# First layer of an eight-stage network: bit unpacking in 16-bit halves, three leaf buffers, codes on VectorE, row sums on TensorE

## The reference, cut to what matters

```python
def fake_quant(x, scale, zp):
    q = jnp.clip(jnp.round(x / scale + zp), 0.0, 255.0)
    return (q - zp) * scale
x = x + jnp.matmul(fake_quant(layernorm(x), s1, z1), fake_quant(ctx, s2, z2))

for p in range(4):                       # plane p holds bit p of each 4-bit code
    bits = (qweight[p][:, :, None] >> shifts & 1).reshape(O, I)
    idx = idx | bits << p
w = jnp.take_along_axis(lut4, idx, axis=1)          # dense weight (512, 512)
x = x + jnp.einsum('bsi,oi->bso', layernorm(x), w) + bias
```

## Time and profile before

| | us |
|---|---|
| median of 3 runs | 890.11 |
| lowest, highest | 885.03, 890.35 |
| the profiled execution, its own time | 884.34 |
| its span in the profile | 882.6 |

### The profile page before, as it was taken

How to read it: one execution, slowest core, us unless ns; L and a number is a source line. 1 busy time by engine, 2 the same in 40 slices (tenths; PEclk the granted TensorE clock), 3 DMA queues, 4 the chain that set the end, 5 groups by cost and what they waited for, 6 DMA issues and landing times. The chain is left out here.

```text
span 882.6 us, 16392 instructions
## 1 busy us (share of the span) xinstructions
PE 784.0 (89%) x5130; PEld 632.8 (72%) x5130; DVE 722.5 (82%) x1712; ACT 518.0 (59%) x1410; POOL 448.2 (51%) x391
## 2 busy tenths in 40 slices
PE   0886699948978899999999999999999999678978
PEld 0366576634657888888888888888888888465446
DVE  7788898977777797897897897897897897974975
ACT  6683788845437557657657657657657657331431
POOL 4727259815134745745745745845844844713110
PEclk9898999989989999999999999999999999989899
DMA  8333146635120320320320320320320320203001
GB/s 313 129 112 116 45 162 213 201 102 168 26 71 1 96 73 1 96 71 0 95 71 0 95 71 0 95 71 0 95 71 0 95 72 0 72 25 116 1 0 48
DMA packets 39114, 68.23 MB, mean 77 GB/s; under 512 B 5729, under 2 KB 18593, under 8 KB 38946
## 3 DMA queue, kind: packets, MB, share of 16 engines
q1 hardware_dynamic: 39074, 67.73, 23.5%
HBM read 62.38 MB, written 5.34 MB: 77 GB/s over the span
## 5 line engine op out<-in xcount | busy, mean ns | idle before, releaser
L2218 DVE TENSOR_SCALAR_CACHE_REDUCE xn<-ctxT,candidate 128x512 bf16<-128x512 f32 x248 | 174.4, 740 | 0.1
L1950 ACT ACTIVATE layer_attention_probs<-xnT,stats 128x512 f32<-128x512 f32 x128 | 93.9, 734 | 135.1 <-DVE stats L2058 135.1
L1734 PE MATMUL bank<-layer_attention_keysT,layer_attention_queriesT 128*128 128x512 f32 x384 | 123.9, 431 | 3.3 <-DVE layer_attention_queriesT L2051 3.3
L2070 DVE TENSOR_TENSOR layer_attention_probsT<-bank,layer_attention_probsT 128x512 fp32r<-128x512 f32 x128 | 88.0, 688 | 40.3 <-ACT layer_attention_probsT L1958 38.9
L1734 PEld LDWEIGHTS bank<-layer_attention_probsT,layer_attention_values 128*128 128x128 f32 x768 | 99.7, 191 | 19.4 <-issue 9.1
L1734 PE MATMUL bank<-layer_attention_probsT,layer_attention_values 128*128 128x256 f32 x768 | 103.1, 284 | 10.3 <-DVE layer_attention_probsT L2070 9.9
L1734 PE MATMUL bank<-layer_attention_wo,layer_attention_headsT 128*128 128x512 f32 x384 | 102.1, 409 | 3.9 <-issue 3.1
L1958 ACT CAST layer_attention_probsT<-bank 128x512 fp32r<-128x512 f32 x128 | 74.7, 584 | 51.1 <-PE bank L1809 51.1
L1681 POOL TENSOR_TENSOR layer_attention_mixed<-layer_attention_mixed,xnT 128x512 f32<-128x512 f32 x32 | 52.3, 1633 | 86.8 <-DMA xnT<-inverse_sums 84.5
L1734 PE MATMUL bank<-layer_attention_l_wq,layer_attention_xnT 128*128 128x512 f32 x384 | 93.7, 393 | 0.7 <-DVE layer_attention_xnT L2119 0.7
L1734 PE MATMUL bank<-layer_attention_l_wkv,layer_context_parts 128*128 128x256 f32 x720 | 90.4, 278 | 0.0
(11 more groups left out here) (318 smaller groups left out, 1690.6 us busy)
## 6 DMA issues: line engine op xcount, KB each, us to landing
layer_attention_l_raw_qo<-in_wqT SPq DMA_DIRECT2D x9, 1024.0 KB, 5.0
xnT<-inverse_sums SPq DMA_DIRECT2D x16, 512.0 KB, 3.7
layer_attention_l_raw_qo<-in_woT SPq DMA_DIRECT2D x8, 1024.0 KB, 7.0
tw_raw<-in_w_gateT SPq DMA_DIRECT2D x8, 688.0 KB, 5.3
tw_raw<-in_w_upT SPq DMA_DIRECT2D x8, 688.0 KB, 4.2
tw_raw<-in_w_downT SPq DMA_DIRECT2D x6, 768.0 KB, 4.7
layer_attention_l_raw_kv<-in_wkvT SPq DMA_DIRECT2D x9, 512.0 KB, 5.0
ternary<-tw_rounded SPq DMA_DIRECT2D x8, 344.0 KB, 2.5
```

The lines of the kernel that those rows point to most:

```text
L1734: last = pe.matmul(out, stationary[f][a], moving[f][b], start=f == 0 and x == 0, stop=f == count - 1 and x == 2)
L1950: a.activation(probs[:, u % 3, :], masked[:, u % 2, :], ACT.Exp, bias=negmax[:, u:u + 1], scale=-1.0, accum_out=sums[:, u:u + 1]).then_inc ...
L2070: v.tensor_tensor(probsT[:, 1, p % 2, :, columns], T[u % 2][:, :].rearrange("p (c q) -> p c q", c=CPB), probsT[:, 0, p % 2, :, columns], A ...
L2218: own(k.nc.vector.tensor_scalar(k.flags[:, r % 2], row_tile(k.ctxT, r), k.candidate[:, r:r + 1].bitcast(F32), 0.0, ALU.is_gt, ALU.add, acc ...
```

## The change

- The packed planes are read as 16-bit halves. `unpack(b)` for b in 0 to 15 takes bit b of every half of all four groups in one shift-and-mask; `bits` is 16-bit, holds all groups at once and is laid out bit-major, and the second norm writes `xn` in the same order of features (`norm_rows(..., HALVES)`). All 16 run before the statistics of x. `shifts`, `moved` and the iota are gone.
- `tree` has three buffers. Leaves: group 0 five by ScalarE and three by GpSimd (ahead of the norm's power in its queue), groups 1 and 2 by ScalarE, group 3 four and four. A small activation loads ScalarE's table early.
- The codes q1 and q2 are made by VectorE, each right behind its rounding. The row sums of the codes come from TensorE (`row_sums`, sixteen products with one column) and not from ScalarE; its rectifying of ctx is interleaved with the copies of q1T.
- The bias is cut into two float32r parts by GpSimd, and added by two products per tile.
- ScalarE's order behind x corrected: leaves(1), weightT_copy(0), leaves(2), xnT copies, leaves(3), wv, first keys copy, then the ternary sums with the weightT copies between them, the second keys copy before sum 7. `keys(1)` is TensorE's last work in the layer, and its two subtractions VectorE's last. `cols` lies in `ctx` and `bias` in `xnT`.

```diff
-def norm_rows(k, n):
+def norm_rows(k, n, halves=None):
...
+        to, source = k.xn[:, t, :], k.x[:, t, :]
+        if halves is not None:
+            to, source = to.rearrange("p (b h) -> p h b", h=halves), source.rearrange("p (h b) -> p h b", h=halves)
...
+    HALVES, HALF_BITS = 2 * WORDS, BITS // 2
+    BUFFERS = 3
+    BY_POOL = {0: 5, 3: 4}
...
+        planes = packed[:, 0:OT * PLANES * WORDS].bitcast(U16).rearrange("p (a h) -> p a h", h=HALVES)
...
-        bits = k.sbuf("bits", [P, 2, PLANES, D], I32, s)
+        bits = k.sbuf("bits", [P, OT, PLANES, D], U16, s)
+        by_bit = bits[:, :, :, :].rearrange("p o a (b h) -> p (o a) b h", h=HALVES)
...
+                    for j in range(BY_POOL[o], CODES // 2):
+                        last = g.tensor_scalar(tree[:, o % BUFFERS, j, :], bits[:, o, 0, :], diff[:, o, j:j + 1],
...
+                leaves(0)
                 norm_gpsimd(k, n)
-                for t in range(TILES):
-                    g.wait_ge(S_["x_rounded"], t + 1)
-                    g.tensor_scalar(q1[:, t, :], k.xn[:, t, :], 1.0, -(ROUND + MIDDLE), ALU.mult, ALU.add)\
-                     .then_inc(S_["q1_ready"], 1)
-                context_codes(0)
-                context_codes(1)
-                leaves(1, 0, CODES // 2, "leaves1_pool")
+                g.wait_ge(S_["bias_loaded"], 16)
+                g.wait_ge(S_["constants_ready"], 5)
+                g.tensor_copy(ones_row[:, :], k.ones[0:1, :]).then_inc(S_["bias_low"], 1)
+                g.tensor_copy(bias_parts[:, 0, :], bias).then_inc(S_["bias_high"], 1)
+                g.wait_ge(S_["bias_high"], 1)
+                g.tensor_tensor(bias_parts[:, 1, :], bias, bias_parts[:, 0, :], ALU.subtract).then_inc(S_["bias_low"], 1)
                 norm_gpsimd(k, n + 1)
-                leaves(3, 0, 4, "leaves3_pool")
+                leaves(3)
...
-                def unpack(o):
...
+                def unpack(b):
+                    v.tensor_scalar(by_bit[:, :, b, :], planes, b, 1, ALU.logical_shift_right, ALU.bitwise_and)\
+                     .then_inc(S_["bits_ready"], 1)
...
-                unpack(0)
+                for b in range(HALF_BITS):
+                    unpack(b)
+                v.wait_ge(S_["bits_ready"], HALF_BITS)
                 v.wait_ge(k.x_loaded, 16)
                 norm_statistics(k)
-                unpack(1)
                 norm_rows(k, n)
                 for t in range(TILES):
...
+                    v.wait_ge(S_["x_rounded"], t + 1)
+                    v.tensor_scalar(q1[:, t, :], k.xn[:, t, :], 1.0, -(ROUND + MIDDLE), ALU.mult, ALU.add)\
+                     .then_inc(S_["q1_ready"], 1)
...
                 norm_statistics(k)
-                unpack(2)
-                norm_rows(k, n + 1)
+                norm_rows(k, n + 1, HALVES)
                 choose(1)
-                unpack(3)
                 choose(2)
                 choose(3)
...
+                keys_low(0)
...
                 tile_norms_vector(k, following, update)
+                keys_low(1)
...
                 a.wait_ge(S_["diff_ready"], 1)
+                a.activation(corr[:, :], lut[:, 0, 0:TILES], ACT.Identity).then_inc(S_["table_loaded"], 1)
                 leaves(0)
...
-                rectified_context(0)
-                rectified_context(1)
...
-                    a.activation(junk[:, t % 2, :], q1[:, t, :], ACT.Copy, accum_out=rows[:, t:t + 1]).then_inc(S_["rows_ready"], 1)
...
+                for t in range(TILES):
+                    rectified_context(t)
+                    if t % 2:
+                        turned_codes(t - 1)
+                        turned_codes(t)
+                for t in range(CPB, CTILES):
+                    rectified_context(t)
...
+                leaves(1)
                 weightT_copy(0)
-                for i in range(3):
-                    ternary_sums_scalar(k, i)
+                leaves(2)
...
-                leaves(2)
-                weightT_copy(1)
-                ternary_sums_scalar(k, 3)
-                leaves(3, 4)
-                ternary_sums_scalar(k, 4)
+                leaves(3)
                 a.wait_ge(lw.ctx_loaded, 32)
                 a.copy(lw.wv[:, :], lw.raw_v[:, :]).then_inc(lw.wv_high, 1)
...
+                keys_copy(0)
+                ternary_sums_scalar(k, 0)
+                weightT_copy(1)
+                ternary_sums_scalar(k, 1)
+                ternary_sums_scalar(k, 2)
                 weightT_copy(2)
-                for i in range(5, 7):
-                    ternary_sums_scalar(k, i)
+                ternary_sums_scalar(k, 3)
+                ternary_sums_scalar(k, 4)
                 weightT_copy(3)
+                ternary_sums_scalar(k, 5)
+                ternary_sums_scalar(k, 6)
+                keys_copy(1)
                 ternary_sums_scalar(k, 7)
...
+                def row_sums():
+                    pe.wait_ge(S_["q1T_ready"], TILES)
+                    for t in range(TILES):
+                        for f in range(KT):
+                            last = pe.matmul(ROWS[:, t:t + 1], q1T[:, f, t * P:(t + 1) * P], ones16[:, 0:1],
+                                             start=f == 0, stop=f == KT - 1)
+                    last.then_inc(S_["rows_psum"], 1)
...
-                        pe.matmul(Y[t][:, :], k.ones[0:1, 0:P], bias[0:1, :], start=True, stop=False, skip_group_check=True)
+                        for part in range(2):
+                            pe.matmul(Y[t][:, :], ones_row[:, :], bias_parts[:, part, :], start=part == 0, stop=False,
+                                      skip_group_check=True)
...
+                row_sums()
                 columns(0)
...
-                pe.wait_ge(S_["weightT_ready"], 1)
-                keys(1)
                 feed_forward(1)
...
                 feed_forward(3)
+                pe.wait_ge(S_["weightT_ready"], OT)
+                keys(1)
```

More of the change, by code:

```diff
@@ L449, in layer0 @@
         d2s = k.sbuf("d2s", [P, 1], F32, s)
-        rows = k.sbuf("rows", [P, TILES], F32, s)
         corr = k.sbuf("corr", [P, TILES], F32, s)
         ones16 = k.sbuf("ones16", [P, P], BF16, s)
-        cols = k.sbuf("cols", [1, B, D], F32, s)
-        junk = k.sbuf("junk", [P, 2, D], BF16, s)
-        shifts = k.sbuf("shifts", [P, BITS], I32, s)
-        moved = k.sbuf("moved", [P, PLANES * WORDS, BITS], I32, s)
-        bits = k.sbuf("bits", [P, 2, PLANES, D], I32, s)
+        cols = ctx[0:1, 0:B, :]
@@ L500, in _ @@
                 g.wait_ge(S_["constants_ready"], 1)
-                def leaves(o, first, end, done):
-                    g.wait_ge(S_["bits_ready"], o + 1)
-                    if o >= 2:
-                        g.wait_ge(S_["weightT_psum"], o - 1)
-                    for j in range(first, end):
-                        last = g.tensor_scalar(tree[:, o % 2, j, :], bits[:, o % 2, 0, :], diff[:, o, j:j + 1],
-                                               lut[:, o, 2 * j:2 * j + 1], ALU.mult, ALU.add)
-                    last.then_inc(S_[done], 1)
@@ L606, in _, with keys_low @@
                 norm_statistics(k)
[L607 to L608 removed]
+                norm_rows(k, n + 1, HALVES)
                 choose(1)
[L610 removed]
                 choose(2)
                 choose(3)
[L613 to L615 removed]
+                def keys_low(b):
                     v.wait_ge(lw.keys_high, b + 1)
@@ L631, in _, with leaves @@
             def _(a):
-                def leaves(o, first=0):
-                    a.wait_ge(S_["bits_ready"], o + 1)
-                    if o >= 2:
-                        a.wait_ge(S_["weightT_psum"], o - 1)
-                    for j in range(first, CODES // 2):
-                        last = a.activation(tree[:, o % 2, j, :], bits[:, o % 2, 0, :], ACT.Identity,
+                def leaves(o):
+                    a.wait_ge(S_["bits_ready"], HALF_BITS)
+                    if o >= BUFFERS:
+                        a.wait_ge(S_["weightT_psum"], o - BUFFERS + 1)
+                    for j in range(BY_POOL.get(o, CODES // 2)):
+                        last = a.activation(tree[:, o % BUFFERS, j, :], bits[:, o, 0, :], ACT.Identity,
                                             bias=lut[:, o, 2 * j:2 * j + 1], scale=diff[:, o, j:j + 1])
@@ L648, in scaled_columns, with rectified_context, turned_codes @@
                     a.activation(cols[0:1, b, :], C[b][0:1, :], ACT.Copy, scale=off[0:1, 0:1]).then_inc(S_["cols_ready"], 1)
-                def rectified_context(b):
-                    a.wait_ge(S_[f"ctx{b}_loaded"], 16)
-                    for t in range(b * CPB, (b + 1) * CPB):
-                        a.activation(ctx[:, t, :], ctx[:, t, :], ACT.Relu, bias=par[:, 3:4], scale=inv[:, 1:2])\
-                         .then_inc(S_["ctx_rectified"], 1)
+                def rectified_context(t):
+                    a.wait_ge(S_[f"ctx{t // CPB}_loaded"], 16)
+                    a.activation(ctx[:, t, :], ctx[:, t, :], ACT.Relu, bias=par[:, 3:4], scale=inv[:, 1:2])\
```

(6 more changed lines are left out.)

88 lines of the change are left out of this document (35 added, 53 removed).

## The result

| | before | changed |
|---|---|---|
| median, us (6 runs each) | 887.08 | 878.31 |
| lowest, highest | 885.03, 890.35 | 876.66, 882.09 |
| profiled execution, its span | 884.34, 882.6 | 877.61, 875.9 |

The ratio is 0.990, with a 95% interval of 0.987 to 0.993. The time lies 6.2 us under the forecast of 884.5 and 0.2 under the low end of the range.

A forecast was written before the change was run, and what follows sets the result against it. The prediction took a chain that changes engine in layer0, the only stage touched, as the bound. Its terms, 2.1 + 1.2 + 3.7 - 1.4 = 5.6 us, took the median from 890.11 to 884.5, range 878.5 to 891.

The forecast's parts named there:

- the anchor: Whole kernel: the median before, 890.11 us, from which the forecast subtracted the saving; the profiled execution lay 5.8 under it.
- part B: Layer0, norm's rows to scaled_columns(1): 1.2 us saved, with TensorE's row sums at 2.1 setting the stage.
- A, start to R: Layer0's opening: 16 unpack operations at 0.23 us and a power without its wait save 2.1 us.
- R: The start of the norm's rows in layer0, forecast at 12.1 us against 14.17 before.
- The rival with the f32 rate: Unpack in layer0's opening at 0.37 us per operation: 2.2 us worse, 886.7; at 0.61, 890.6; chance 0.18.
- C, to the last products: Layer0, scaled_columns(1) to the last products: ScalarE's 23.5 us, then waits for ternary pieces; 3.7 us saved.
- D, to layer1: Last products to layer1: keys(1)'s two subtractions now stand behind the norm; 1.4 us lost.
- The mask: Rival: VectorE's choosing gets slower from a 16-bit mask for f32 data; at double price 895.3 us; chance 0.06.
- the clock's: Rival: TensorE's products before layer1 run at clock 0.50, up to 3.8 us more per group, 892; chance 0.06.
- The length from layer1 on: Sign: everything from layer1 on shifts whole; a change by more than 2 us would show the prediction wrong.
- the three open prices: Row sums (limited to 1.4 us), fetches under 4.0 (0.8 at most) and layer1's first transposes less cold (1.2).
- TensorE's side goes better: Rival: row sums, fetches and layer1's first transposes all cheaper, 9.0 us saved, 881.1; chance 0.2.

The follow-up runs named there:

- e5_unpack_strided: The changed kernel with its 16 unpack operations stepping innermost over the 16 planes, not along the halves: 893.84 us, ratio 1.0075 to the kernel before.
- e2_bias_late: The changed kernel with GpSimd's three bias operations held back until the first group's weight is chosen: 879.03 us, ratio 0.9885 to the kernel before.
- e3_copies_first: The changed kernel with ScalarE's weightT copies 1, 2 and 3 each one ternary sum earlier: 877.87 us, ratio 0.9865 to the kernel before.
- e8_keys_before: The changed kernel with keys(1), its copy and its subtractions back before feed_forward(1): 879.61 us, ratio 0.9890 to the kernel before.
- e9_bias_f32: The changed kernel with the bias added by one f32 product per tile again: 881.60 us, ratio 0.9939 to the kernel before.
- e12_busy: The changed kernel with bias operations late, weightT copies earlier and unused products on TensorE while it waits: 878.80 us, ratio 0.9855 to the kernel before.

## Why the prediction was right and wrong

The result lies 6.2 us under the forecast, and outside the range. The chain of engines was right. What failed is the anchor, the median that the forecast was hung on, and in part B the price of TensorE's row sums (2.1 us, measured 0.59) and the place of GpSimd's bias work; another part of the gap stays open.

**The anchor, 3.0 us.** The forecast was hung on the median of three runs, 890.11; six runs gave 887.08, and 887.56 to 892.62 beside the later experiments. The text had the profiled execution 5.8 under its median as a warning of that and took it for a constant.

**Layer0, 1.6 us.** It gained 7.2 in place of 5.6 in the profiled execution. In the two others it gained 7.2 and 5.2, so the 1.6 are within what one kernel's layer0 varies by; on the mean of the three, 6.5, the forecast is 0.9 short. Term by term, for the first execution:

- A, start to R: 2.45, forecast 2.1. The bound taken for the unpack, 0.23 us, was right and a little high; measured 0.207. The power's 3.34 us was a wait indeed, 1.03 is left. The rival with the f32 rate is out. That the price comes from the dense 16-bit form is argued; e5_unpack_strided shows only that it needs the dense form.
- B, R to the last scaling: 1.95, forecast 1.2. The mis-sized term is the row sums: sixteen one-column products at 0.13 each, 2.1 us, from a row of 12-column ones; they take 0.59, 0.037 each. Columns(0) so starts at R+9.6 and not R+10.7, 1.1 earlier, though it then waits 0.20 for a code of VectorE: the sums no longer set it. Attention's products, half of them 0.43 us apart, took 2.82 in place of 2.3 and gave some of that back. The bias work was priced, "by 1.5, partly in that wait", but put beside the codes of ctx, where it had cover; it struck x's rows of the norm, on the path, and cost 0.8 (e2_bias_late).
- C, to the last products: 4.19, forecast 3.7. The chain was right in order and in length: ScalarE's 23.5 us came out as 22.85 to the end of weight copy 1 at 49.56, the first fetch took 4.07 (issued 49.12, summed from 53.19) for the 4.0, and the last products stood behind a ternary piece as forecast. In this trace TensorE had turned groups 2 and 3 at 53.89 and 59.44 and the copies came at 54.54 and 60.21, so the waits cost 0.65 and 0.77; the forecast had 0.8 for both together. The 2.0 us of e3_copies_first are this and the length of sum 0.
- D, to layer1: 1.37 lost, forecast 1.4. e8_keys_before gives 10.27 back for 10.29. That keys(1) was free in its new place was right. What the prediction didn't price is the other side: moving it frees 3.6 us of TensorE ahead of the last products. With that, the traces have the old place 0.3 to 1.6 us better in all, so most of the 1.4 is paid back.
- The mask: the predicated copies of 2048 elements took 2462 ns in the mean with the 16-bit mask, and 2466 in the kernel before. That rival is out too, and so is the clock's: the last products took 3.84 us, as before.
- keys(0) and the bias were said to be hidden, ScalarE reaching the xnT copies at R+31. It reached them at R+29.8, 1.2 us behind the end of keys(0) and 0.35 behind that of the first eight turns (40.12 + 1.04), and e9_bias_f32 and e12_busy show that the cover is gone when the bias grows by 1.7 us, or bias and keys(0) together by 1.6. The conclusion held, by little.

**What is left, 1.6 us.** The medians differ by 8.8 where layer0 differs by 7.2. Over three comparisons they differ by 9.2 in the mean (8.8, 11.6, 7.2), and layer0's end in three profiled executions by 7.2, 7.2 and 5.2 from the one of before. So some 2 to 3 us are seen in the medians and not located in a trace. The likeliest reading is that the profiled execution of before was one of its short ones: it lies 2.7 under its own six-run median, and its stretch of columns and attention, 5.03, is shorter than in every execution of the changed kernel. With one trace of before that is argued, not shown; the cause of this part stays open. The length from layer1 on, whose change by more than 2 us the prediction took for a sign of being wrong, is no such sign: one and the same kernel had 803.4 and 807.6.

**The range** held the three open prices together as one case at 881.1 and half of the runs' spread under it, 878.5. Hung on 887.08 the same working would have given 881.5 as forecast and 875.5 to 888 as range, with the result inside. The width was enough for that, and the place was off.

**The chances.** 0.76 stood on a change within 1%. The first comparison gives 0.990, the others 0.9886 and 0.9915: it is on that bound, between the two cases. A layer0 gain of 7.2 is the forecast with half of the rival "TensorE's side goes better"; the row sums, one of its three prices, did fall that way. The other two did not: the fetch took 4.07, and layer1's first transposes 3.66 in place of 3.79. So the nearness of 7.2 to that rival is in part luck.

## What to carry to other kernels

When a chain crosses engines, price each operation also for what it does to the neighbour: a short operation on GpSimd beside VectorE's row work can land on the path, and a sum queued in front of a weight copy costs its own length and the wait for its transfer. Look at more than one execution before a microsecond is given a cause: the same kernel showed layer0 at 72.5 and 74.5 us. And take the anchor of a forecast from as many runs as there are, since three of them were 3 us off here.

## What the runs showed of the hardware that was not expected

- TensorE's pace at the opening varies between executions of one kernel. Products of 512 bf16 columns came 0.43 us apart (1.2 GHz) from columns(0) on, and 0.21 apart (2.4 GHz) from a moment between 24.6 and 26.5 us, though the granted clock in the windows of that stretch reads 1.00. What the engine did before decides, by one execution: with extra products while it waited, they ran at the full pace from the start (e12_busy); in the thirteen other traces of these products none did, and in e5_unpack_strided no transfer ran beside them. The Trainium skill (TensorE: Matmul & The Clock Gate, What's actually happening) has a gate that sets the clock by how busy the array has lately been, with the point of transition varying from run to run; in the pace of the products the traces agree, in the granted clock of this stretch they don't show it.
- Sixteen products with one column and a new 128x128 bf16 stationary operand each took 0.59 us, 0.037 each. The Trainium skill (TensorE: Matmul & The Clock Gate, "Wait — 56ns, not 53.3ns?") has about 25 ns from start to start as the least, however few the columns; the measured price is half as much again.
- Work on a single partition holds up the neighbour too: GpSimd's operations on 1x512 elements took 0.80 and 1.32 us and lengthened VectorE's four rows from 1.91 to 3.16 (e2_bias_late undoes it).
- A dense shift-and-mask from 16 to 16 bits over 512 elements costs 0.207 us from one start to the next; with an innermost step of 64 bytes in the source and 1 KiB in the result 1.12 us.
